# A recurrence on one core: where PE visits the loop's code, what fills the gate's gaps, who loads b, and when a chunk is stored

## The reference

```
h    = silu(q_pool @ W1.T + b1)
gate = sigmoid(h @ W2.T + b2)
...
xW = einsum('ntd,dh->nth', x, Wx) + b
def step(prev_h, xw):
    next_h = tanh(prev_h @ Wh + xw)
...
x = x + _L1_cond_ref(x, cond_1024, Wx, Wh, b)
```

## Time and profile before

| | us |
|---|---|
| median of three runs | 197.02 |
| the profiled execution | 196.62 |
| its span, first to last instruction | 194.8 |
| PE busy | 176.0 (90%) |
| ACT busy | 85.3 (44%) |
| DVE busy | 98.2 (50%) |
| loop, from the first tanh (10.18) on | 184.6 |

### The profile page before, as it was taken

How to read it: one execution, slowest core, us unless ns; L and a number is a source line. 1 busy time by engine, 2 the same in 40 slices (tenths; PEclk the granted TensorE clock), 3 DMA queues, 4 the chain that set the end, 5 groups by cost and what they waited for, 6 DMA issues and landing times.

```text
span 194.8 us, 33383 instructions
## 1 busy us (share of the span) xinstructions
PE 176.0 (90%) x15962; PEld 167.4 (86%) x15962; DVE 98.2 (50%) x395; ACT 85.3 (44%) x518; POOL 0.5 (0%) x5
## 2 busy tenths in 40 slices
PE   4899999999999999999999999999999999999995
PEld 2698988988898898889889889888988988898895
DVE  0445465455546545555554654555465455545543
ACT  3234444444444444444444444444444444444442
POOL 1000000000000000000000000000000000000000
PEclk9999999999999999999999999999999999999999
DMA  6309999702020020202002020200202020020212
GB/s 200 109 30 320 397 415 406 294 1 108 0 107 3 0 109 0 108 0 107 1 2 108 0 109 0 106 2 2 108 0 108 0 100 9 0 109 0 108 54 54
DMA packets 7105, 17.98 MB, mean 92 GB/s; under 512 B 1459, under 2 KB 2867, under 8 KB 7094
## 3 DMA queue, kind: packets, MB, share of 16 engines
q1 hardware_dynamic: 6656, 17.32, 23.8%
q10 hardware_dynamic: 438, 0.55, 0.8%
HBM read 9.48 MB, written 8.39 MB: 92 GB/s over the span
## 4 chain that ended last, share of the span: by engine, by line
PE 86%; ACT 7%; issue 3%; DMA 3%; SPq 0%
PE bank_e L193 48%; PE bank_l L193 38%; ACT h_ring L178 7%; DMA w_t<-in_w 3%; SPq L129 0%
## 5 line engine op out<-in xcount | busy, mean ns | idle before, releaser
L193 PE MATMUL bank_e<-h_ring,wh_sb 128*32 128x32 f32 x4096 | 98.6, 204 | 13.5 <-ACT h_ring L178 13.5
L178 ACT ACTIVATE h_ring<-bank_e 128x32 f32<-128x32 f32 x256 | 50.5, 197 | 101.7 <-PE bank_e L193 101.7
L193 PE MATMUL bank_l<-h_ring,wh_sb 128*32 128x32 f32 x4096 | 91.2, 196 | 0.0
L193 PEld LDWEIGHTS bank_e<-h_ring,wh_sb 128*32 128x32 f32 x4096 | 71.5, 108 | 20.2 <-ACT h_ring L178 20.1
L193 PE MATMUL bank_l<-x_ring,wx_sb 128*32 128x32 f32 (+1 forms) x4112 | 81.0, 200 | 0.0
L341 DVE TENSOR_TENSOR x<-x,h_ring 128x128 f32<-128x128 f32 x129 | 37.6, 291 | 84.0 <-ACT h_ring L178 84.0
L193 PE MATMUL bank_e<-x_ring,wx_sb 128*32 128x64 f32 (+1 forms) x2056 | 71.0, 224 | 0.0
L193 PEld LDWEIGHTS bank_l<-h_ring,wh_sb 128*32 128x32 f32 x4096 | 69.8, 113 | 0.0
L193 PEld LDWEIGHTS bank_l<-x_ring,wx_sb 128*32 128x32 f32 (+1 forms) x4112 | 64.5, 111 | 0.0
L193 PE MATMUL bank_l<-ones,b_sb 128*32 128x32 bf16 (+1 forms) x1026 | 51.7, 180 | 0.0
L178 ACT ACTIVATE h_ring<-bank_l 128x32 f32<-128x32 f32 x256 | 50.4, 197 | 0.0
(11 more groups left out here) (31 smaller groups left out, 14.0 us busy)
## 6 DMA issues: line engine op xcount, KB each, us to landing
x<-in_x SPq DMA_DIRECT2D x15, 512.0 KB, 9.5
out_dram<-x SPq DMA_DIRECT2D x15, 512.0 KB, 3.5
w_t<-in_w SPq DMA_DIRECT2D x1, 256.0 KB, 5.4
wx_sb<-in_wx SPq DMA_DIRECT2D x1, 256.0 KB, 5.7
wh_sb<-in_wh ACTq DMA_DIRECT2D x1, 256.0 KB, 5.0
x<-in_x SPq DMA_DIRECT2D x1, 256.0 KB, 3.1
out_dram<-x SPq DMA_DIRECT2D x1, 256.0 KB, 2.5
w_t<-in_w_cond ACTq DMA_DIRECT2D x1, 145.0 KB, 3.8
```

Of the source, the lines that this page charges most:

```text
L178: nc.scalar.activation(h_ring[:, m, s * B:(s + 1) * B], z_of(s, m), ACT.Tanh)\
L193: done = nc.tensor.matmul(out[q:q + columns], weights[:, q:q + columns], moving, start=start, stop=stop, skip_group_check=True)
```

## The change

PE's branch to the visit moves from behind the first fillers to behind the bias products, and waits for Wx first. The first filler has six matmuls in place of three, and its wait is for both `one` and `ones`, which DVE now sets in that order. The two-column-tile fillers between the gate's layers stay what they were, under another name. Step 0 is laid in another order: the first half of x times Wx for both m, then for each m the start state times Wh and the second half of x. POOL issues b's rows in place of ACT. A chunk is stored at a count one higher, which is one pair of steps later; the last chunk's five pieces stay.

```diff
-        STORES = [(c, 0, CS, (c + 1) * CS // 2) for c in range(CHUNKS - 1)]
+        STORES = [(c, 0, CS, (c + 1) * CS // 2 + 1) for c in range(CHUNKS - 1)]
...
         @block.gpsimd
         def _(pool):
             nc.gpsimd.memset(b_parts, 0.0).then_inc(b_cleared, 1)
+            pool.wait_ge(b_cleared, 2)
+            pool.dma_start(b_sb[32:97:32, :, :], b_rows).then_inc(b_loaded, DMA)
...
             act.dma_start(x_head[:], x_first).then_inc(x_head_loaded, DMA)
-            act.wait_ge(b_cleared, 2)
-            act.dma_start(b_sb[32:97:32, :, :], b_rows).then_inc(b_loaded, DMA)
             act.dma_start(wh_sb[:], wh).then_inc(wh_loaded, DMA)
-            act.wait_ge(ones_ready, 1)
+            act.wait_ge(ones_ready, 2)
...
-            pe.wait_ge(ones_ready, 1)
-            warm_up(3)
-            nc.br("pe_visit", engines=only_pe)
-            stage = nc.switch_bb("pe_first_stage")
+            pe.wait_ge(ones_ready, 2)
+            keep_busy(6)
...
             pe.wait_ge(b_loaded, DMA)
-            pe.wait_ge(one_ready, 1)
             lay_whole_bias(0, 2, 0)
             lay_whole_bias(0, 1, 1)
+            pe.wait_ge(wx_loaded, DMA)
+            nc.br("pe_visit", engines=only_pe)
+            stage = nc.switch_bb("pe_first_step")
+            pe.wait_ge(first_input_ready, 1)
+            for m in range(HALVES):
+                lay_input(0, 1 if m else 2, 0, m, columns=64)
             pe.wait_ge(wh_loaded, DMA)
-            for k in range(HALVES):
-                for m in range(HALVES):
+            for m in range(HALVES):
+                for k in range(HALVES):
                     recur(0, k, m, cond_t[:, k, :], columns=64)
-            for k in range(HALVES):
-                pe.wait_ge(first_input_ready, k + 1)
-                if k == 0:
-                    pe.wait_ge(wx_loaded, DMA)
-                for m in range(HALVES):
-                    done = lay_input(0, 1 if m else 2, k, m, columns=64)
-                    if k == HALVES - 1:
-                        done.then_inc(z_whole[m], 1)
+                if m == 0:
+                    pe.wait_ge(first_input_ready, 2)
+                lay_input(0, 1 if m else 2, 1, m, columns=64).then_inc(z_whole[m], 1)
...
             with nc.body("pe_visit", parent=stage.parent, valid_engines=only_pe):
-                warm_up(1, 32)
-                nc.br("pe_first_stage", engines=only_pe)
+                keep_busy(1, 32)
+                nc.br("pe_first_step", engines=only_pe)
...
-            nc.vector.memset(ones[:], 1.0).then_inc(ones_ready, 1)
-            nc.vector.memset(one[:], 1.0).then_inc(one_ready, 1)
+            nc.vector.memset(one[:], 1.0).then_inc(ones_ready, 1)
+            nc.vector.memset(ones[:], 1.0).then_inc(ones_ready, 1)
```

More of the change, by code:

```diff
@@ L97, in build @@
         ones_ready = sem("ones_ready")
-        one_ready = sem("one_ready")
         b_cleared = sem("b_cleared")
@@ L182, in _, with keep_busy @@
         def _(pe):
-            def warm_up(n, columns=512):
+            def keep_busy(n, columns=512):
                 for _ in range(n):
@@ L195, in by_columns, with keep_busy_by_columns @@
                 return done
-            def keep_warm(n):
-                for _ in range(n):
-                    by_columns(idle_ps, ones[:], ones[:, 0:1].to_broadcast([P, 512]), start=True, stop=True, columns=64)
+            def keep_busy_by_columns():
+                by_columns(idle_ps, ones[:], ones[:, 0:1].to_broadcast([P, 512]), start=True, stop=True, columns=64)
             def gate_product(layer, k, m, w_t, operand):
@@ L236, in _ @@
                 done.then_inc(z1_product, 1)
-            keep_warm(1)
+            keep_busy_by_columns()
             for k in range(HALVES):
```

## The result

| | before | after |
|---|---|---|
| median of 21 runs each, us | 196.45 | 195.33 |
| lowest to highest | 195.74 to 197.21 | 194.77 to 196.93 |
| the profiled execution | 196.62 | 195.19 |
| ratio | | 0.9962, 95% interval 0.9945 to 0.9979 |

The change makes the kernel faster, by 0.77 us between the means (196.47 and 195.70). I had forecast 2.19. The three runs shown ahead (197.0) lay in the upper part of the spread of the kernel before, 0.55 us over the mean of its 21 runs, so that much of the way from 197.02 to 195.33 is not the change's; the ratio does not depend on it.

What follows compares the result with a forecast made beforehand. PE was taken to bound the kernel, its chain beginning with W2's landing. Terms -1.2 + 0.45 - 1.1 - 0.49 + 0.15 = -2.19 took the median 197.02 to 194.8 us; range 193.8 to 196.5.

Steps and rivals of the forecast that it cites:

- The loads: Ahead of the loop: code packet and b leave the loads' way, second layer at 5.5 in place of 6.72, -1.2 us.
- b by POOL: Ahead of the loop: POOL's transfer must be there by 6.7, and one microsecond later than ACT's still fits; nothing.
- The visit on the path: Between bias and inputs: PE's branch out, return and one small matmul, hidden in a wait before, cost +0.45 us.
- The rival in which the visit stalls for the fetch: At the visit's branch PE waits until the code has come: 3.7 in place of 0.45, 199.0 us; chance 0.07.
- The clock: Ahead of the loop: PE runs at 2.4 GHz from the visit on, halving 2.17 us of products, -1.1 us.
- The store: In the loop: storing a chunk one pair later saves 0.035 us at each of 14 chunk ends, -0.49 us.
- Turn 0: At the loop's second block, whose code the visit fetches: PE has less time before reaching it, +0.15 us.

Runs made afterwards that it cites:

- first experiment: The changed kernel with only the visit put back behind the six first fillers: 195.95 us (12 runs), ratio 0.9967 to the kernel before.

## Why the prediction was right and wrong

**The loads: right.** The packet belongs to the visit (first experiment), W2 lands 1.83 us earlier, and silu bounds the second layer, at 5.08 where I had 5.5: -1.64 against -1.2. That the first tanh came near the forecast (-2.02 against -1.85) is in part luck, since the way from the second layer to it gave 0.38 and not 0.65, by the waits for b and Wx.

**b by POOL, taken as nothing: wrong.** I asked only that it be there by 6.7 on my own schedule; with the second layer at 5.08 the bias was wanted at 5.86, b landed at 6.14, and Wx came at 6.66 where it came at 5.46 to 5.74 with b on ACT. About +0.5, where the level rises early.

**The visit on the path: the size was near.** PE stands still for 0.45 us between the bias and the visit's matmul, which is the size that I gave to the gap, but in after the wait for Wx has a part in it: PE's queue ran empty during it, and nothing hid the branch. Where Wx had landed and the queue was full (b by ACT, first profile), the visit's matmul and the first input start 0.13 apart and nothing stands still. The rival in which the visit stalls for the fetch is refuted: the visit's matmul came at 7.06, before the packet began at 7.90. By the Trainium skill (Runtime: NRT & Kernel Launch, Instruction fetch mechanics) a taken branch outside the resident pages stalls until the code is fetched. At the visit the branch took 0.31 us, as before, so this trace shows no such stall. A wait for code did appear, in turn 0 and without a taken branch, where PE ran on from the loop's first block into the next.

**The clock: right in kind, wrong as a certainty.** In the profiled execution of after the level rose within the second layer, which ran from 5.08 on, even earlier than the visit. But after's runs divide: thirteen below 195.6 with mean 195.17 (1.3 us under the mean of before, 196.47) and eight from 195.92 to 196.93 with mean 196.55, no gain at all. Averaged, 13/21 x 1.3 = 0.8. I read one profile, saw one rise behind four microseconds of products without a break, and gave it to every execution. In the execution of b by ACT at 196.81, PE worked from 3.76 to past 13 with no gap over 0.12 us, and at 12.39 a step still took 1.067. This is the first step that failed: the term of -1.1, and with it most of the earlier first tanh, holds in part of the executions only. If the level is low in turn 0, a step there takes 1.067 and gives back what the loads gained, as with three fillers. That after's two groups are these two levels is concluded from its variants (four repeated profiles, and the one with the old store count); no execution of after's upper group was profiled.

**The store: wrong, and the second step that failed.** -0.49 forecast, 0 measured, at two places and with the stores gone from the loop. The long step belongs to every fourth jump back, whatever stands beside it. The 14 coincidences with a store, one of which stands in the earlier trace rows (turn 8, beside turn 9 without), had the same period as the chunks, four turns, and that was all that joined them: in other profiles, three of one program among them, the long steps stand at other turns of a chunk. I had the counter-evidence: pieces issued at other branches cost nothing.

**Turn 0: mis-sized, the third.** +0.15 forecast, +0.63 measured. The term named the code behind the first block, and that wait is real (0.18 us in after, 0.68 and 0.88 in two variants), but in the profiled execution of after x's second piece ended last, 0.38 later, and my sum had no term for it.

For the profiled execution: -2.02 + 0.63 - 0.02 = -1.41, against my -2.19. The store makes 0.47 of the gap and turn 0 0.48, the start gives back 0.17. Of the rest of the miss, from -1.41 to the -0.77 between the means, 0.53 is the executions in which the clock stays low (-1.30 without them); the remaining 0.11 is how the two profiled executions lie to their means.

## What to carry to other kernels

On a kernel of 200 us with a start of 10, look at the single times before you price a clock: two groups 2 us apart are one program at two levels, and a median says mainly how often each came. The version in which the high level was the rule had seven fillers from 0.78 us on, and the break of the visit where another engine's work was waited for anyway: 14 of its 15 executions (with both places of the store) lay at 194.03 to 194.84. The fillers alone left a median of 195.4, the place of the visit alone two groups at 194.2 to 194.7 and 196.5 to 196.8.

That a long step comes back with the period of something else names no cause: move the suspect alone, or look at a second profile, before you pay for it. And what moves out of the way of one load (the packet, b) comes back in front of another (turn 0, Wx).

## What the runs showed of the hardware

- A packet of 16 KB of PE's code takes 0.92 to 1.5 us of one DMA engine, and a load that it falls among lands later (W2 at 6.06 to 6.66 us in three profiles, at 4.57 to 5.14 in those without the packet there). PE could use the code 1.4 to 1.5 us after the packet's end (three profiles). The branch to the visit took 0.31 us in every profile and the return 0.17; the packet began 1.0 to 2.8 us behind that branch.
- Every fourth jump back of PE's loop takes 0.319 us instead of 0.273 from the branch's start to the next instruction (0.312 instead of 0.266 in after and two other profiles), in all 18 profiles, at a turn of the four that differs between profiles, of one program too; why is open.
- The level of the clock can fall back ahead of the loop although PE was busy for two thirds of the time and paused for 0.5 us at most (granted 1.00, then 0.50 for 6.8 us). In a profile without such a change the column reads 1.00 also where products take the time of the lower level: durations decide. The Trainium skill (TensorE: Matmul & The Clock Gate, HAM oscillation) tells of falls when PE waits for DMA between bursts of products. The trace agrees in kind, since both falls here came behind waits for b and Wx, but these were of 0.35 to 0.49 us only, and after waited 0.33 and 0.45 without a fall.
- b's 6 KB landed at 6.14 to 7.00 us when POOL issued them and at 5.22 to 5.56 when ACT did, and with the visit late Wx was later with POOL too (6.11 to 6.88 against 5.46 to 5.74).
